# Where four pieces of the ternary FFN weights stand in GpSimd's order in batch 0, and where SyncE moves the fourth unit's second maxima

## The reference

```
q, k, v = x Wq' + bq, x Wk' + bk, x Wv' + bv        # 16 heads of 16
q, k    = rope(q) / 4, rope(k)
a       = softmax(q k') v                            # per head, 1024 x 1024 scores
x       = layernorm(x + a Wo' + bo)
Wt1, Wt2 = ternary(W1), ternary(W2)                  # clip(round(W / (mean|W| + 1e-5)), -1, 1)
x       = layernorm(x + relu(x Wt1' + b1) Wt2' + b2) # hidden width 1024
```

## Time and profile before

| | us |
|---|---|
| median of 3 runs (lowest, highest) | 3300.49 (3297.68, 3303.40) |
| the profiled execution's own time | 3303.37 |
| its span in the trace | 3301.6 |
| busy: PE / DVE / ACT / POOL | 98% / 91% / 77% / 65% of the span |
| granted TensorE clock, mean | 0.988 of full speed |

### The profile page before, as it was taken

One profiled execution on the slowest core, in us unless ns is written; L12 is line 12 of the kernel. 1 busy time (PEld: TensorE's weight loads), 2 busy tenths in 40 slices (PEclk: granted clock), 3 DMA queues, 4 the chain that ended last, 5 costly groups with the idle time before them and its releaser, 6 DMA issues. The chain is left out here.

```text
span 3301.6 us, 82481 instructions
## 1 busy us (share of the span) xinstructions
PE 3248.1 (98%) x31190; PEld 1786.8 (54%) x31190; DVE 2990.3 (91%) x5721; ACT 2532.8 (77%) x4971; POOL 2149.4 (65%) x2440
## 2 busy tenths in 40 slices
PE   6999999999999999999999999999999999999997
PEld 4444555555555555555555555555555555555546
DVE  7889999999999999999999999999999999999965
ACT  3777777777777777777777777777777777777773
POOL 2575766766766766766766766766766766754444
PEclk7999999999999999999999999999999999999999
DMA  8444354454354354354454354354354354354211
GB/s 215 108 99 105 92 116 103 98 116 109 91 116 108 93 116 107 93 116 104 97 116 109 92 116 107 93 116 108 92 116 105 95 116 107 93 110 86 57 42 54
DMA packets 312557, 341.27 MB, mean 103 GB/s; under 512 B 77280, under 2 KB 260448, under 8 KB 312160
## 3 DMA queue, kind: packets, MB, share of 16 engines
q1 hardware_dynamic: 311584, 335.20, 44.4%
q10 hardware_dynamic: 576, 0.79, 0.2%
HBM read 195.37 MB, written 140.51 MB: 102 GB/s over the span
## 5 line engine op out<-in xcount | busy, mean ns | idle before, releaser
L1074 DVE TENSOR_REDUCE mxp<-ms 128x1 f32<-128x512 f32 x4064 | 2617.6, 683 | 232.2 <-PE ms L749 186.5
L900 ACT ACTIVATE prob<-sc 128x512 f32<-128x512 f32 x4096 | 2225.5, 597 | 634.3 <-PE sc L760 607.3
L760 PE MATMUL sc<-qa,ka 50*128 50x512 f32 x4096 | 1543.3, 445 | 4.3 <-DMA qa<-maxima 3.4
L749 PE MATMUL ms<-ka,qa 48*128 48x512 f32 x4064 | 1537.3, 446 | 2.9 <-DVE mxp L1292 2.2
L760 PEld LDWEIGHTS sc<-qa,ka 50*128 50x128 f32 x4096 | 688.9, 185 | 1067.9 <-ACT prob L900 918.8
L777 PE MATMUL ob<-prob,v_sb 128*17 128x512 f32 (+1 forms) x8656 | 1094.2, 577 | 2.7 <-ACT at_st L907 2.4
L749 PEld LDWEIGHTS ms<-ka,qa 48*128 48x128 f32 x4064 | 684.1, 185 | 10.0 <-DVE mxp L1074 3.9
L1405 POOL TENSOR_TENSOR ve<-mv,eps_sb 128x2 f32<-128x2 f32 x119 | 23.4, 197 | 492.8 <-DVE mv L1101 492.8
L1426 POOL TENSOR_TENSOR hid_r<-hid,hid_r 128x512 fp32r<-128x512 f32 x240 | 308.7, 1286 | 19.2
L777 PEld LDWEIGHTS ob<-prob,v_sb 128*17 128x17 f32 x8656 | 143.7, 95 | 273.5 <-issue 273.2
L597 PEld LDWEIGHTS job<-h_t,w_sb 64*128 64x128 f32 x3840 | 261.0, 186 | 23.7 <-issue 0.6
(11 more groups left out here) (157 smaller groups left out, 2843.3 us busy)
## 6 DMA issues: line engine op xcount, KB each, us to landing
qk_parts<-parts SPq DMA_DIRECT2D x122, 512.0 KB, 4.3
ka<-qk_parts SPq DMA_DIRECT2D x378, 128.0 KB, 4.7
qa<-qk_parts SPq DMA_DIRECT2D x378, 128.0 KB, 7.4
attention<-at_st SPq DMA_DIRECT2D x128, 256.0 KB, 3.0
v_ones<-v_st SPq DMA_DIRECT2D x64, 272.0 KB, 2.4
v_sb<-v_ones SPq DMA_DIRECT2D x64, 272.0 KB, 8.4
xn<-x SPq DMA_DIRECT2D x64, 256.0 KB, 4.8
ao<-attention SPq DMA_DIRECT2D x128, 128.0 KB
```

The costliest lines, as they stand in the source:

```text
L749: nc.tensor.matmul(ms[upto(b, g, NS1, at) % MS_BANKS][:, :], operand(qa, b, g, j, ROWS)[:, qt * P:(qt + 1) * P], operand(ka, b, g, j, ROWS ...
L760: nc.tensor.matmul(sc[upto(b, g, HG * STEPS, n) % SC_BANKS][:, :], operand(ka, b, g, j, ROWS + MROWS)[:, tt * P:(tt + 1) * P], operand(qa, ...
L900: nc.scalar.activation(prob[st_ % 2][:, j, :], sc[upto(b, g, HG * STEPS, n) % SC_BANKS][:, :], ACT.Exp).then_inc(s["exp_done"], 1)
L1074: nc.vector.reduce_max(mxp[(b * G + g) % 2][:, kh, j * TT + qt:j * TT + qt + 1], ms[upto(b, g, NS1, at) % MS_BANKS][:, :], AX.X).then_inc( ...
```

## The change

In unit (0, 2) GpSimd makes three pieces of W1 where it made four. The fourth, and the first two of W2, come at the end of the unit. The last two pieces of W2 move to unit (0, 3), behind its `add_products`. SyncE in unit (0, 3) moves the second half's maxima before it waits for the ternary pieces, not after the load of `xn`. The rest of the kernel is as it was; every operation is still done once.

```diff
@@ SyncE, unit @@
                 if (b, g) == (0, G - 1):
+                    move_maxima(b, g, 1)
                     sp.wait_ge(s["ternary_done"], 2 * TERNARY_PIECES)
                 if prepared(b, g)[0] >= 0:
                     tail_in(*prepared(b, g))
-                move_maxima(b, g, 1)
+                if (b, g) != (0, G - 1):
+                    move_maxima(b, g, 1)
@@ GpSimd, unit, behind add_products of the first projection @@
                 if (b, g) == (0, 2):
-                    for piece in range(TERNARY_PIECES):
+                    for piece in range(TERNARY_PIECES - 1):
                         ternary(0, piece)
+                elif (b, g) == (0, G - 1):
+                    for piece in range(2, TERNARY_PIECES):
+                        ternary(1, piece)
@@ GpSimd, unit, behind split_x of the next projection @@
                 if (b, g) == (0, 2):
-                    for piece in range(TERNARY_PIECES):
-                        ternary(1, piece)
+                    ternary(0, TERNARY_PIECES - 1)
+                    ternary(1, 0)
+                    ternary(1, 1)
```

## The result

| | before | changed |
|---|---|---|
| median of 17 runs each, us | 3302.98 (3296.83 to 3305.96) | 3308.31 (3301.27 to 3312.84) |
| the profiled execution, us | 3303.37 | 3303.39 |
| span of its trace, us | 3301.6 | 3301.6 |

The ratio is 1.0019, with a 95% interval of 1.0011 to 1.0026. It takes in all runs and isn't that of the two medians, which is 1.0016. The changed kernel is slower by 0.19%, a little over the +0.13% (4.25 us) of the sum, and just inside the 0.2% that I called no change. Behind the first hunk of the diff, lines of the changed kernel stand two further down: L760 is now L762, L1129 is L1131. In e2 and e7 they stand four further down, in e9 two or three.

What follows compares the result with a forecast made beforehand. TensorE (98% busy) and VectorE (91%) bound the kernel, so any delay of either counts whole. Gains of 2.74 and 3.31 us against a 6.6 us stall and 3.7 of clock gave +4.25, forecast 3305 us, range 3298.5 to 3310.

Steps and rivals of the forecast that it cites:

- the sum: Whole kernel: -2.74 - 3.31 + 6.6 + 3.7 = +4.25 us, from the old stall and clock gained, new stall and clock paid.
- rival C: Unit (0, 3): the `den` load lands late and lengthens TensorE's stall; up to +7.5 us, 3308.0; chance 0.17.
- Part 1: Three W1 pieces ahead of unit (0, 2)'s maxima: TensorE's 2.67 us stall and the half clock go, gaining 6.05 us.
- Part 2: Three pieces end unit (0, 2): `rotate_even` about 1 us late, covered since `rotate_odd` waits for VectorE until 236.1.
- Part 3: Unit (0, 3): SyncE moves the maxima ahead of the wait, four DMAs at 234.4, no cost, 4.1 us to spare.
- Part 4: Unit (0, 3): late W2 pieces delay store and `den`; VectorE's inversion waits S = 6.9 us, TensorE stalls 6.6.
- The clock behind the new gap: Behind unit (0, 3)'s step 11 stall: 10 us at half clock, costing 3.7 us, bounds nothing and 4.0.
- A: Rival, unit (0, 3): the inversion doesn't stall, so the gain of 6.05 us stands alone, 3294.4; chance 0.07.
- B: Rival, unit (0, 3): the stall comes but the clock stays up, +0.55 us, 3301.0; chance 0.12.
- D: Rival, start of unit (0, 3): the change doesn't remove the first stall, +10.3 us, 3310.8; chance 0.04.

Runs made afterwards that it cites:

- e2: The changed kernel, but SyncE waits for the pieces and loads `xn` behind `attention_in` instead of ahead of it; 3296.98 us, 0.9987 of before.
- e7: e3, but SyncE moves the maxima of unit (1, 0) ahead of the chain of reciprocals; 3300.62 us, 1.0000 of before.
- e9: e1, but in units (0, 2) and (0, 3) ScalarE copies the previous unit's attention outputs whole, not in halves; 3289.92 us, 0.9965 of before.
- e1: The changed kernel, but GpSimd makes the last two W2 pieces right behind unit (0, 3)'s second `split_maxima`; 3295.54 us, 0.9980 of before.
- e4: GpSimd's part of the change alone, with SyncE in the order of before; 3314.13 us, 1.0034 of before.
- e5: SyncE's part of the change alone, with GpSimd's order as before; 3300.97 us, 0.9997 of before.
- e6: The changed kernel, but unit (0, 3)'s two W2 pieces stand between `rotate_odd` and `add_products`; 3302.06 us, 1.0003 of before.
- e8: The changed kernel run and traced once more, beside others on the same chip; 3305.27 us, 1.0019 of before.
- e3: The changed kernel, but unit (0, 3)'s VectorE inversion stands behind step 14, part 0, not step 10, part 3; 3301.72 us, 1.0001 of before.
- e10: e1 once more, beside e9 on the same chip; 3295.61 us, 0.9983 of before.

## Why the prediction was right, point by point

The range that was given, 3298.5 to 3310 around 3305, held the 3308.31; the sum had +4.25 us and the medians moved by 5.3. Of the 3.3 us between 3305 and 3308.31, 2.5 are the base: the median of before's first three runs was 3300.49, that of all 17 is 3302.98. So it means nothing that the absolute time stands at rival C's 3308.0.

- *Part 1, the stall goes and is worth 6.05 us.* Right. The maxima were issued at 211.92 (211.88 by the sum), and e1 gives 6.1 us under before and D = 93.04 for the 93.0 worked out.
- *Part 2, a late `rotate_even` is covered.* Right: `rotate_odd` began at 236.34, still after 1.68 us of idle time that VectorE ended.
- *Part 3, four DMAs at 234.4, at no cost.* Right; they were issued at 234.69. e4 shows what the kernel pays without it.
- *Part 4, the store waits for the pieces and VectorE for `den`.* Right in place and cause, and near in size: `xn` at 253.05 for 252.85, `den` at 257.47 for 256.3, its landing 2.0 us later at 259.47 for 258.5, S 7.58 for 6.9, TensorE's gap 6.91 for 6.6. Two of its terms were off, and partly made up for each other. The store behind two other transfers took 3.47 us for 2.55. And TensorE's gap is shorter than VectorE's wait by 0.67 us where the sum had 0.3; in e5, e6 and e8 the difference is 0.65 to 0.66. e2, e3 and e6 took away the queue's wait, VectorE's wait and more than half of the delay, and the gap followed each time.
- *The clock behind the new gap, 3.7 us.* Too much. The level and the length (10 us) were right, but part of the time at half is the gap itself, where it costs nothing. The changed kernel paid 56.0 - 46.5 - 6.91 = 2.5 us, e8 2.7. Even that may not be the clock alone: by the prediction's own rate, 0.37 us for each at half, the 5.5 us behind the gap cost 2.0. The reading of the earlier trace rows was also a little off: a mean of 0.59 in the microsecond from 231 puts the clock's return at 231.8, not 231.4, and before was at half for 10.2 us, not 10.6. It moves no term.
- *The sum.* By place: -2.74 - 3.31 + 6.91 + 2.5 = +3.4 us, which is the 3.45 of the traces. The runs say 5.3 by medians, and 3.6 to 8.6 by the interval of the ratio. So the +3.45 stands just under that interval, and 0.2 to 5 us of the difference between the kernels are in no trace. The sum took it that every run of before pays the 6.05. The two traces with this gap, before and e5, both have the fall behind it; whether each run has is not known. The forecast's lower bound of +3.2 doesn't come out of its terms either: the stall of 5.9 with 3.7 for the clock gives +3.55.

Of the rivals, A fell by the wait itself, B by the 0.50, and D by the score tile at 218.27. C has the right direction, but S stayed under its 9.2, and what came late was the store, not the landing, which took 2.0 us.

The section of the Trainium skill on HAM oscillation (TensorE: Matmul & The Clock Gate), which is the clock's fall and return behind one wait after another, was weighed against the earlier trace rows: by the rule a moved stall pays its clock price again, by the row it might not. The runs agree with the rule in every kernel with a gap of over 2 us in step 8 or 11: in the change, e4, e6 and e8 U is 2.5 to 2.9 us longer than 46.5 and the gap together.

## What to carry to other kernels

Before moving work on one engine, list what the queue behind the next wait for it carries: here 4.5 us less on GpSimd's path to the maxima, worth 6.1 us, was paid back with a gap of 6.9 us and its clock, because the wait for the moved pieces stood ahead of a store that VectorE needed ten steps into the unit. Give a wait for late work a place behind what others need sooner (e2), or do the work early enough that the wait is over when the queue comes to it (e1); both took the loss away. And where single executions scatter by as much as the change is worth, compare traces by place, not by span.

## What the runs showed of the hardware that I had not expected

- A gap of TensorE of 1.3 us was followed by the half clock in two of the eleven traces that have this gap in unit (0, 2), those of e2 and e4; the other nine, before and the change among them, show 1.00 there. In the nine traces that have it in unit (0, 3) too, at full clock, it was never followed by a fall. In e2 and e4 the half clock lasted 6.8 us and made unit (0, 2) 2.8 us longer. The 3.21 us gap of the earlier trace rows had none.
- Episodes at half clock differ in length: 20.5 us in e4 around its gap of 14.89, 10.2 in before, the change, e5 and e8, 6.8 in e6 and e7, and 3.4 in e3 with its gap of 4.61. In e3 the clock fell at 266.9, just before the gap ended, and was back within two steps:

```profile
266.00:268.00 2.00, 0.82 (x4) 0.73 (x6) 0.00 (x0) 0.00 (x0) 0.00 (x0) 0.72 0.63 188
268.00:270.00 2.00, 2.00 (x12) 1.56 (x12) 1.29 (x2) 1.08 (x2) 0.00 (x0) 0.50 1.03 343
270.00:272.00 2.00, 2.00 (x18) 0.71 (x16) 1.29 (x2) 1.33 (x3) 0.00 (x0) 0.93 1.12 272
```

- A store of 256 KB took 2.03 to 2.05 us to the next issue that waits for it in before, e1, e2, e4 and e10, 3.24 to 3.90 directly behind two loads of 256 KB (the change, e3, e6, e7, e8), and 4.34 once (e5) with none just ahead.
